# Text front end of a two-layer gated cross-attention kernel: mask plan first, queries for active tiles, key norms spread over later stages

## The chip, the core and the metric

The kernel runs on one core of one Trainium2 chip. The metric is the device time of one execution in microseconds (us). Three runs of the kernel before took 568.72, 568.03 and 567.38 us, median 568.03.

## What is computed

The activations `x` are 16 batches of 56 tokens of 128 numbers (896 tokens); the context `ctx` is 16 batches of 1500 keys of 128. Cut to what matters:

```
x = x + tanh(g_xattn[0]) * A0(layernorm(x), ctx, kv_mask, q_mask)
x = x + tanh(g_ffn[0])   * E0(layernorm(x))          # 16 experts, top 4, plus a shared one
x = x + tanh(g_xattn[1]) * A1(layernorm(x), ctx)     # slot attention, 3 iterations, GRU
x = x + tanh(g_ffn[1])   * E1(layernorm(x))          # 32 experts, top 2, capacity 68

A0:  q, k, v = x Wq, ctx Wk, ctx Wv                  # 16 heads of 64
     s = where(q_mask[i] & kv_mask[j], q k^T / 8, -max)
     out = softmax(s) v Wo + bout
A1:  keys are divided by rms(key) = sqrt(mean(key^2) + 1e-6)
```

Only a pair (query, key) that is set in both masks has a score of its own. The masks are the complements of random lengths, so few pairs are set. A query without any such key attends to all 1500 keys alike: its output is the mean of the keys through `Wv Wo`. So A0 needs three things of the context: the keys of the active blocks, the mean key of each batch, and (for A1 later) the sum of squares of every key.

## The kernel before

All of it is one program with one instruction stream for each engine, written out by hand, and semaphores between them. The order on an engine is the order of the code.

**Folding.** `Wq Wk^T` of each of the 16 heads is multiplied once (L1455, 32 matmuls of 64 rows, evicted by ACT in L785) into `G`, and `Wv Wo` into `MO`; `MS` is the sum of `MO` over the heads, a reduction on DVE (L1050). The weights arrive by four DMAs in `ld_attn`, and PE waits for all four.

**Layernorm.** `ln(k)` (L956 to L967 on DVE, L766 and L768 on ACT, L1429 to L1441 on PE) takes means by a matmul, subtracts, squares, takes variances by 14 one-column matmuls, a square root, a reciprocal, a diagonal matrix and a matmul that broadcasts it. The front end waits for all 28 constants that POOL writes (L594 to L632).

**Front end (L1443 to L1487 on PE).** After `ln(0)` and the folds, a loop over 16 steps `b` does two things at once. For head `b` it computes the queries of all 896 tokens (L1469, two halves of 448 columns, evicted by ACT, L791) into `tilesT`. For batch `b` the keys are loaded into one of four buffers `mctx` (L507, L532 to L536), POOL adds the 12 chunks of a row to six (L639) and to three (L642), PE sums them over the partitions (L1464), ACT squares all of them (L776, 1536 columns), and DVE reduces the squares (L996). The buffers, `msq` (two) and the semaphores `key_sq`, `key_ss`, `key_add`, `key_sum` tie these together.

**Plan.** Queries are cut in tiles of 8 tokens (7 tiles a batch), keys in 4 blocks of 375. A pair (tile of a batch, block) that has a set query and a set key is an *item*. DVE finds them between the key reductions: L1004 to L1015 (counts), L1018 to L1034 (lists), L1039 to L1041 (one-hot rows `hot_r`), and PE multiplies lists by one-hot rows at `b == 6` (L1484). The results (`item_bt`, `item_blk`, `item_dst`, the number of items and of tiles) are written at L1056 to L1063. The masks come by eight DMAs on SP's queue (L518, L519), behind seven loads of activations, weights and context.

**Items (L1510 to L1526 on PE).** A loop of two items a trip, two items ahead. For item `j` PE does: transpose of the probabilities of `j` (L1515), scores of `j+2` (L1498, and the mask by L1499), transpose of the result of `j-1` (L1504), and the product with the values of `j` (L1523). ACT: eviction of the transposed probabilities (L832), exponentials of `j+2` (L807, L808), eviction of a result (L815), and it also issues the DMA for the rows of item `j+1` (L820). DVE: `block_maximum(j+2)` (L1077, L1079, L1082, L1084), then `accumulate(j)` (L1088, L1091, L1093, L1097). POOL copies the 8 queries of 16 heads (L658) and makes the mask row (L659). SP loads the transposed keys (L544, L545). Loads have two buffers.

**Behind the items.** The output projection over the active tiles (L1541), `ln(1)`, the gate and 18 steps of layer 0's experts (L1561, L1570, L1595 on PE, L848 on ACT, L1178 and L1182 on DVE), the square root of all 192 columns of `sumsq` (L838) and its reciprocal (L1168), `ln(2)`, then layer 1. From `x_new` 2 on SP loads the keys of the first eight batches, transposed (L568) and plain (L572) in turn.

## Time and profile before

| quantity | us |
|---|---|
| three runs | 567.38, 568.03, 568.72 |
| the profiled execution | 568.96 |
| its span in the profile | 567.2 |
| PE busy in the span | 479.8 (85%) |
| DVE busy | 358.0 (63%) |
| ACT busy | 321.6 (57%) |
| POOL busy | 210.8 (37%) |

The profile is of one execution. A view of stretches gives each engine's busy time between two moments, with the granted clock of PE (1.00 is 2.4 GHz, half of that 1.2 GHz). A timeline lists instructions by start. A view of groups gives, for each line and engine, busy time, mean duration, and the idle time in front of it with what ended it. PEld is PE's loading of weights. A name ending in q is an engine's queue: what it issues or waits for.

### The profile page before, as it was taken

Reading aid. Unit: us, or ns where it says so; the run is one execution under the profiler, and the core shown is the slowest. Engines: PE = TensorE matmul, PEld = TensorE weight load, DVE = VectorE, ACT = ScalarE, POOL = GpSimd, SP = SyncE. Lnnn points to the kernel's source line nnn. Section 1 sums busy time; section 2 is a strip of 40 time slices with the busy share of each in tenths; the row PEclk is TensorE's granted clock in tenths of the full one; section 3 lists DMA queues with packets and bytes.
Section 4 is the critical chain, followed back from the end, with each engine's and each line's share of the span. In section 5 each row is a group of like instructions: output and inputs, shape, how many; then the busy total and the mean of one; then the engine's idle time right before and its main releaser. Section 6 shows DMA issues by size and latency. Waiting matters only on the chain.

```text
span 567.2 us, 17702 instructions
## 1 busy us (share of the span) xinstructions
PE 479.8 (85%) x6484; PEld 364.5 (64%) x6484; DVE 358.0 (63%) x1029; ACT 321.6 (57%) x959; POOL 210.8 (37%) x366
## 2 busy tenths in 40 slices
PE   4894988999796999879999998999998588489980
PEld 2531225566573454458999987899997458479980
DVE  0789964677627354458889888788888544023333
ACT  2564763555411122379999999899999240033330
POOL 8293862222420000034555445445544203602331
PEclk9996996999797799999999999999999988879996
DMA  8762643444149970600000498000000596120013
GB/s 333 251 222 97 209 165 101 136 138 141 48 160 418 356 93 1 259 40 2 4 3 17 185 365 319 4 4 3 0 0 3 200 426 283 50 78 21 26 31 106
DMA packets 30566, 75.17 MB, mean 133 GB/s; under 512 B 6669, under 2 KB 22078, under 8 KB 29486
## 3 DMA queue, kind: packets, MB, share of 16 engines
q1 hardware_dynamic: 26062, 62.47, 32.1%
q0 software_dynamic: 1424, 7.81, 3.7%
q10 hardware_dynamic: 3024, 4.13, 2.2%
q8 instruction: 38, 0.62, 0.5%
q14 instruction: 18, 0.15, 0.1%
HBM read 69.85 MB, written 4.54 MB: 131 GB/s over the span
## 4 chain that ended last, share of the span: by engine, by line
PE 39%; ACT 20%; DVE 18%; issue 8%; POOL 7%; DMA 5%; ACTq 1%; POOLq 1%; DVEq 0%; SPq 0%
ACT work L864 14%; PE ps L1561 5%; PE ps L1762 4%; PE ps L1469 4%; PE ps L1776 3%; PE ps L1595 3%; DVE ps L1200 2%; POOL xe_scratch L751 2%; PE ps L1423 2%; POOL rq L696 2%; PE ps L1616 2%; PE ps L1541 2%; DMA region<-in_ctx_blk 2%; PE ps L1644 2%; ACT work L881 2%
## 5 line engine op out<-in xcount | busy, mean ns | idle before, releaser
L864 ACT ACTIVATE work<-ps,nb,rkey 125x56 f32<-125x56 f32 x576 | 179.6, 514 | 4.6 <-DVE nb L1208 4.4
L1630 PEld LDWEIGHTS ps<-work,region 128*61 128x61 f32 (+1 forms) x2304 | 75.2, 136 | 8.2 <-issue 5.0
L1630 PE MATMUL ps<-work,region 128*61 128x56 f32 (+1 forms) x2304 | 76.3, 221 | 4.1 <-ACT work L864 3.7
L1644 PE MATMUL ps<-region,work 125*64 125x129 f32 x1152 | 73.5, 274 | 3.2 <-POOL work L715 1.9
L715 POOL TENSOR_TENSOR work<-work,rs 125x336 f32<-125x336 f32 x96 | 70.6, 756 | 3.8
L1644 PEld LDWEIGHTS ps<-region,work 125*64 125x64 f32 x1152 | 64.8, 136 | 4.6 <-POOL work L715 2.6
L1217 DVE TENSOR_REDUCE sm<-work 125x6 f32<-125x336 f32 x96 | 45.5, 492 | 17.5 <-ACT work L864 17.5
L1200 DVE TENSOR_REDUCE ps<-ps 125x6 f32<-125x336 f32 x96 | 44.4, 504 | 0.8 <-PE ps L1630 0.7
L1616 PE MATMUL ps<-GI,work 112*64 112x112 f32 (+3 forms) x288 | 34.7, 309 | 5.8 <-DVE work L1264 3.1
L708 POOL TENSOR_TENSOR rs<-rs,rkey 125x12 f32<-125x12 f32 x48 | 10.3, 215 | 75.7 <-DVE rs L1226 75.7
L1469 PE MATMUL ps<-xln,folded 128*128 128x448 f32 x64 | 29.9, 592 | 10.0 <-ACT region L791 10.0
L848 ACT ACTIVATE early_w<-ps 128x448 f32<-128x448 f32 (+1 forms) x18 | 9.8, 543 | 43.2 <-PE ps L1561 43.2
L757 POOL DMA_INDIRECT ys_scratch<-folded,yidx x17 | 16.3, 957 | 45.2 <-ACT folded L935 42.5
L776 ACT ACTIVATE region<-early_w 125x1536 f32<-125x1536 f32 x16 | 23.7, 1490 | 12.8 <-DVE sumsq L996 12.8
L639 POOL TENSOR_TENSOR region<-early_w 125x768 f32<-125x768 f32 x16 | 29.0, 1813 | 4.8 <-DMA early_w<-in_ctx 3.4
L996 DVE TENSOR_REDUCE sumsq<-region 125x12 f32<-125x1536 f32 (+1 forms) x16 | 27.7, 1746 | 3.3 <-ACT region L776 3.3
L1561 PE MATMUL ps<-xln,early_w 128*128 128x448 f32 x64 | 29.8, 595 | 0.0
L1469 PEld LDWEIGHTS ps<-xln,folded 128*128 128x128 f32 x64 | 11.3, 197 | 26.8 <-ACT region L791 19.3
L1178 DVE TENSOR_TENSOR early_w<-early_w,ps 128x448 f32<-128x448 f32 (+1 forms) x18 | 11.1, 619 | 23.5 <-ACT early_w L848 23.5
L807 ACT ACTIVATE early_w<-m_before,m_minus 128x1 f32 (+1 forms) x22 | 6.5, 295 | 31.8 <-DVE m_minus L1084 31.8
L1616 PEld LDWEIGHTS ps<-GI,work 128*64 128x64 f32 (+2 forms) x288 | 17.2, 134 | 11.4 <-issue 4.1
L642 POOL TENSOR_TENSOR work<-region 125x384 f32<-125x384 f32 x16 | 16.0, 999 | 20.2 <-PE ps L1464 19.1
(303 smaller groups left out, 999.2 us busy)
## 6 DMA issues: line engine op xcount, KB each, us to landing
region<-in_ctx_wide SPq DMA_DIRECT2D x16, 774.0 KB, 7.0
early_w<-in_ctx SPq DMA_DIRECT2D x16, 768.0 KB, 4.3
region<-in_w SPq DMA_DIRECT2D x6, 2048.0 KB, 19.8
region<-in_ctxT SPq DMA_DIRECT2D x16, 750.0 KB, 9.2
work<-in_ctxT_blk SPq DMA_DIRECT2D x22, 187.5 KB
early_w<-in_w POOLq DMA_DIRECT2D x1, 4096.0 KB, 12.4
region<-in_ctx_blk ACTq DMA_DIRECT2D x11, 192.0 KB, 2.8
early_w<-in_ctx_blk ACTq DMA_DIRECT2D x10, 192.0 KB, 2.5
```

The lines of the kernel that those rows point to most:

```text
L639: gp.tensor_tensor(padd6[:CP, :], mctx[k][:CP, 0:CC // 2 * 128], mctx[k][:CP, CC // 2 * 128:], ALU.add).then_inc(key_add, 1)
L715: gp.tensor_tensor(shares_of(p, a, h), shares_of(p, a, h), bcast(rs[:, a, c], S), ALU.mult).then_inc(a_att, 1)
L776: act.activation(msq[k % 2][:CP, :], mctx[k][:CP, :], ACT.Square).then_inc(key_sq, 1)
L864: i = act.activation(shares_of(p, a, h)[:, c, :], ps[:CP, 2 + 2 * h + a, c * S:(c + 1) * S], ACT.Exp, bias=nb[:, a, q:q + 1], scale=rkey[: ...
L996: v.tensor_reduce(sumsq[:, bass.ds(b, 1), :], msq[k][:CP, :].rearrange("p (a c d) -> p a c d", a=1, d=D), AX.X, ALU.add).then_inc(key_ss, 1)
L1200: v.tensor_reduce(ps[:CP, 2 + 2 * h + a, 400:400 + CH], ps[:CP, 2 + 2 * h + a, 0:CH * S].rearrange("p (c s) -> p c s", s=S), AX.X, ALU.max ...
L1217: v.tensor_reduce(sm[:, a, c], shares_of(p, a, h), AX.X, ALU.add).then_inc(a_sum, 1)
L1469: pe.matmul(ps[:, h, 0:HALF], G[:, b, :], xln[:, half(h)], start=True, stop=True).then_inc(qa_mm, 1)
L1561: mm = pe.matmul(ps[:p, 2 * (j % 2) + g, 0:HALF], w, xln[:, half(h)], start=True, stop=True)
L1616: mm = pe.matmul(out[r0:r1], w[:, r0:r1], x, start=start, stop=stop, **more)
L1630: mm = pe.matmul(ps[r0:r1, 2 + 2 * h + a, c * S:(c + 1) * S], keysT[:, s, c0 + r0:c0 + r1], qT[:, p, a * S:(a + 1) * S], start=True, stop= ...
L1644: mm = pe.matmul(ps[i * COL:(i + 1) * COL, bank, 0:KW], A[:CP, p % 2, i, h, c * S:c * S + COL], keys[:, 2 * p + i, h * CH + c, :], start=( ...
```

## The change

Constants: the loads of items get a ring of four buffers (`RING`), the first 16 items are written out (`FIRST`), and eight batches are `MEAN_ONLY` in the front end.

1. SP's queue starts with `xT`, the weights of the first fold, four batches, then the weights of the second fold. The eight mask loads are issued by ACT on its own queue. ACT runs a `Sqrt` on one column before its first wait for all constants.
2. PE's first means wait for one constant instead of 28. DVE makes the counts of the plan inside `ln(0)`, after the centring, and the one-hot rows before the last step of `ln(0)`; PE does folds and the rank matmuls in between. The lists follow `ln(0)`.
3. Queries are computed for one tile at a time, for the tiles that have items only (`head_queries(i, tile)`: 16 matmuls of 128 columns, four evictions of 512). The last tile is done always, the others in a loop over `tiles`.
4. POOL adds a batch once, to six chunks; the second addition is gone, and PE sums with two matmuls of 384 columns instead of one. Sums for batches 0 to 7 are in the front end, squares for none.
5. The second fold (`MO`) comes after the queries, straight before the items, and `MS` comes from eight matmuls instead of DVE's reduction.
6. Between items 0 to 15, batches 8 to 15 are worked on: at even `j` POOL's addition and ACT's squares, at odd `j` DVE's reduction of them and PE's sums. The two matmuls of `keep_d` and the scaling that follows are behind items 1 and 2. The reduction to `mean_rows` is behind the items. ACT issues no DMAs for items; SP does. The DMAs of `w13` and `w2p` are behind item 15 on POOL.
7. In the first 16 steps of layer 0's experts, ACT squares half a batch (768 columns) of the keys that layer 1 has loaded (`msq0`), and DVE reduces it one step later. The square root for these eight batches stands in front of `ln(2)` on ACT, the reciprocal inside `ln(2)` on DVE. SP loads all plain keys of the first eight batches before the transposed ones. POOL's `key_rms` is behind `x_new` 4.
8. Layer 1's late expert weights are waited for eight experts at a time instead of four.

```diff
@@ SP
+            for dst, name in ((wqT, "wqT"), (wkT, "wkT")):
+                sp.dma_start(dst, t[name]).then_inc(ld_attn[0], 16)
+            for k in range(KEY_BUFS):
+                load_batch(mctx[k], k, ld_mctx[k])
+            for dst, name in ((wvT, "wvT"), (wo, "wo")):
+                sp.dma_start(dst, t[name]).then_inc(ld_attn[1], 16)
...
+            for b in range(KEY_BUFS, MEAN_ONLY + 2):
+                load_later(b)
+            sp.wait_ge(items_ok, 2)
...
+            for j in range(FIRST):
+                if j == 2:
+                    sp.wait_ge(fold_mm, 9)
+                blk = block_of(j)
+                load_keysT(blk, j, j % RING)
+                load_rows(blk, j, j % RING)
+                if j in LOAD_AFTER:
+                    load_later(LOAD_AFTER[j])
...
@@ POOL
+            def key_adds(b):
+                k = b % KEY_BUFS
+                gp.wait_ge(ld_mctx[k], b // KEY_BUFS * 16 + 16)
+                gp.wait_ge(key_sum, b + 1)
+                gp.tensor_tensor(padd6[b % 2][:CP, :], mctx[k][:CP, 0:CC // 2 * 128], mctx[k][:CP, CC // 2 * 128:], ALU.add).then_inc(key_add, 1)
...
+            for j in range(FIRST):
+                item_queries(j + AHEAD, (j + AHEAD) % RING, (j + AHEAD) // RING * 32 + 32)
+                if j in SQUARES_AT:
+                    key_adds(SQUARES_AT[j])
...
@@ ACT
+            for r in range(TILES):
+                act.dma_start(km8[r * B:(r + 1) * B, 0:M], t["kv_mask"]).then_inc(ld_mask, 16)
...
+            act.activation(warm_up[:, :], eps_ln[:, :], ACT.Sqrt)
             act.wait_ge(const, CONSTS)
             ln(0)
...
+            def item(j, k):
+                act.wait_ge(pt_mm, j + 1)
+                act.wait_ge(o_mm, j + 4)
+                act.copy(PT[:KP].rearrange("p c r -> p (c r)"), ps[:KP, 2, 0:KC * 128]).then_inc(pt_ev, 1)
+                probabilities(j + AHEAD, k % 2)
+                keep_result(j)
...
+            for j in range(FIRST):
+                item(j, j % RING)
+                if j in SQUARES_AT:
+                    squares(SQUARES_AT[j])
...
+                if j < HALVES:
+                    act.wait_ge(ld_keys[j // 4], 32)
+                    act.wait_ge(key_ss, B - MEAN_ONLY + j + 1)
+                    act.activation(msq0[j % 2][:CP, :, :], keys[:, j // 2, half_batch(j), 0:D], ACT.Square).then_inc(key_sq, 1)
...
@@ DVE
+            ln(0, plan_counts, plan_places)
...
+            v.wait_ge(plan_list, 2)
...
+            v.sem_inc(items_ok, 1)
...
+            for j in range(FIRST):
+                block_maximum(j + AHEAD, j % 2)
+                if j in SUMS_AT:
+                    key_squares(SUMS_AT[j])
+                accumulate(j)
+                if j == 2:
+                    keep_scales()
...
@@ PE
+            ln(0, first_folds)
+            for q in range(2, 4):
+                fold(0, q)
+            pe.wait_ge(plan_rs, 1)
...
+            for b in range(2):
+                key_sums(b)
...
+                    for m in range(4):
+                        mm = pe.matmul(ps[:, q % 2, m * 128:(m + 1) * 128], G[:, 4 * q + m, :],
+                                       by_tile(xln[:, :])[:, tile, :, :], start=True, stop=True)
+                    mm.then_inc(qa_mm, 1)
...
+            pe.wait_ge(plan, PLAN_LISTS)
...
+            for b in range(2, 5):
+                key_sums(b)
+            head_queries(0, TILES - 1)
+            for b in range(5, 7):
+                key_sums(b)
             pe.wait_ge(items_ok, 1)
...
+            with pe.Fori(1, tiles) as i:
+                head_queries(i, bass.ds(pe.snap(TILES - 1 - i), 1))
+            key_sums(MEAN_ONLY - 1)
...
+            for pair in range(H // 2):
+                mm = pe.matmul(ps[:, ALL_BANK, 0:128], wvT[:, pair, :], wo[:, pair, :], start=(pair == 0), stop=(pair == H // 2 - 1))
+            mm.then_inc(fold_mm, 1)
+            for q in range(4):
+                fold(1, q)
+            pe.wait_ge(fold_ev, 9)
...
+            for j in range(FIRST):
+                item(j, j % RING, j // RING * 32, j // RING * 16)
+                if j in SUMS_AT:
+                    key_sums(SUMS_AT[j])
...
```

## Rows read from the trace of the kernel before

**Rows 1.** Stretches: from:to, length, then busy us of PE, PEld, DVE, ACT, POOL, granted clock.
```profile
50.00:83.90 33.90, 30.50 (x82) 10.54 (x83) 29.13 (x28) 24.47 (x33) 20.14 (x18) 0.94 0.55 183
...
83.90:147.20 63.30, 57.63 (x286) 36.45 (x286) 42.33 (x164) 31.44 (x102) 20.14 (x46) 0.92 0.46 131
```

**Rows 2.** Timeline of the front end (start us, duration us; in brackets idle before, releaser).
```profile
7.17 3.35 PE L1429 MATMUL ps<-xT,mean_w 128*128 128x448 f32 x4 [7.17 <-POOL before_b L632]
...
9.88 1.28 ACT L766 ACT_TABLE_LOAD   x1 [9.75 <-DVE ln_tiles L956]
...
11.80 3.15 PE L1434 MATMUL ps<-mean_w,ln_tiles 128*128 128x1 f32 x14 [1.28 <-ACT ln_tiles L766]
...
34.22 1.11 DVE L1018 TENSOR_SCALAR firstc<-prefix 112x4 f32<-112x4 f32 x1
...
46.48 0.21 DVE L1034 TENSOR_SCALAR lists_w<-btidx,lastc 112x1 bf16<-112x1 f32 x1
```

**Rows 3.** The key mask's loads on SP's queue: issue to landing, min/median/max.
```profile
DMA to landing us min/median/max: 7.2/8.1/9.0
```

**Rows 4.** Groups of the front end: busy us, mean ns | idle before, releaser.
```profile
L639 POOL TENSOR_TENSOR region<-early_w 125x768 f32<-125x768 f32 x16 | 29.0, 1813 | 4.8 <-DMA early_w<-in_ctx 3.4 <-POOL before_b L632 0.4
...
L996 DVE TENSOR_REDUCE sumsq<-region 125x12 f32<-125x1536 f32 (+1 forms) x16 | 27.7, 1746 | 3.3 <-ACT region L776 3.3
...
L776 ACT ACTIVATE region<-early_w 125x1536 f32<-125x1536 f32 x16 | 23.7, 1490 | 12.8 <-DVE sumsq L996 12.8
...
L1464 PE MATMUL ps<-work,early_w 125*16 125x384 f32 x32 | 13.1, 491 | 0.7 <-ACT folded L785 0.7
...
L1030 DVE CAST first_w<-firstc 112x128 bf16<-112x128 f32 x4 | 5.7, 1417 | 0.0
...
L1455 PE MATMUL ps<-region 64*128 64x128 f32 x64 | 5.3, 289 | 0.0
```

**Rows 5.** Timeline: first scores, first and last transposes of items, output projection.
```profile
83.91 0.87 PE L1498 MATMUL ps<-work 128*128 128x375 f32 x2 [2.21 <-POOL work L659]
...
87.35 1.00 PE L1515 MATMUL ps<-GI,work 128*125 128x128 f32 x3
...
144.10 0.49 PE L1515 MATMUL ps<-GI,work 128*125 128x128 f32 x3
...
152.27 9.46 PE L1541 MATMUL ps<-region,folded 128*128 x64
```

**Rows 6.** Timeline of items in their steady state, three engines.
```profile
124.86 0.29 ACT L807 ACTIVATE early_w<-m_before,m_minus 128x1 f32 x1 [0.96 <-DVE m_minus L1084]
...
125.70 0.27 ACT L815 COPY region<-ps 128x128 f32 x1
...
125.78 0.33 PE L1499 MATMUL ps<-work,ones_b 1*128 1x375 bf16 x1
...
126.16 0.48 ACT L832 COPY work<-ps 125x384 f32<-125x384 f32 x1 [0.18 <-issue]
...
126.29 0.23 DVE L1077 SCALAR_TENSOR_TENSOR m_before<-m_run,work 128x1 f32<-128x1 f32 x1 [0.48 <-PE ps L1499]
...
126.77 0.93 PE L1523 MATMUL ps<-region,work 125*128 125x128 f32 x6 [0.19 <-ACT work L832]
...
127.08 0.16 DVE L1082 TENSOR_TENSOR m_run<-m_block,m_before 128x1 f32<-128x1 f32 x1
...
127.53 0.49 PE L1515 MATMUL ps<-GI,work 128*125 128x128 f32 x3
...
127.56 0.29 ACT L807 ACTIVATE early_w<-m_before,m_minus 128x1 f32 x1 [0.92 <-DVE m_minus L1084]
...
128.59 0.33 PE L1499 MATMUL ps<-work,ones_b 1*128 1x375 bf16 x1
```

**Rows 7.** Timeline of layer 0's experts (a step of DVE) and of ACT in ln(2).
```profile
198.30 0.62 DVE L1178 TENSOR_TENSOR early_w<-early_w,ps 128x448 f32<-128x448 f32 x1 [1.17 <-ACT early_w L848]
...
232.34 1.26 ACT L766 ACTIVATE ln_tiles<-ln_tiles 128x448 f32<-128x448 f32 x2 [0.80 <-DVE ln_tiles L956]
```

More of the change, by code:

```diff
@@ L32 @@
 AHEAD = 2
+RING = 4
+FIRST = 16
+MEAN_ONLY = 8
+SQUARES_AT = {2 * k: MEAN_ONLY + k for k in range(B - MEAN_ONLY)}
+SUMS_AT = {2 * k + 1: MEAN_ONLY + k for k in range(B - MEAN_ONLY)}
+LOAD_AFTER = {0: 10, 1: 11, 5: 12, 7: 13, 9: 14, 11: 15}
+FOLD_BANK = ((4, 5, 6, 3), (4, 5, 6, 3))
+ALL_BANK = 0
+SUM_BANK = 7
+HALVES = 2 * MEAN_ONLY
 E0, F0, TOP0, ROUTE = 16, 64, 4, 2.5
@@ L283, in build_program @@
         ld_x = sem("ld_x")
-        ld_attn = sem("ld_attn")
+        ld_attn = [sem(f"ld_attn{f}") for f in range(2)]
         ld_small = sem("ld_small")
@@ L801, in _ @@
+            head_queries(0, TILES - 1)
+            act.wait_ge(items_ok, 1)
+            tiles = act.value_load(item_n[0:1, 1:2], min_val=2, max_val=TILES)
+            with act.Fori(1, tiles) as i:
+                head_queries(i, bass.ds(act.snap(TILES - 1 - i), 1))
+            act.wait_ge(fold_mm, 5)
+            act.copy(MS[:, :], ps[:, ALL_BANK, 0:128]).then_inc(fold_ev, 1)
+            for q in range(4):
+                fold(1, q)
             act.wait_ge(ld_small, 16 * SMALL)
@@ new lines, in plan_places @@
+            def plan_places():
+                v.wait_ge(plan_rs, 1)
+                step(v.tensor_reduce(bidx[:, :], bstep[:, :], AX.X, ALU.add))
+                step(v.scalar_tensor_tensor(btidx[:, :], bidx[:, :], -float(B), btidx[:, :], ALU.mult, ALU.add))
+                for b in range(KB):
+                    step(v.tensor_scalar(lists_w[:, b, 3:4], bidx[:, :], -1.0, float(TILES), ALU.mult, ALU.add), wait=False)
+                v.wait_ge(plan_rank, 2)
+                step(v.tensor_scalar(rank[:, :], prefix[:, :], ps[:BT, 2, 0:1], None, ALU.add))
+                for b in range(KB):
+                    v.tensor_scalar(hot_r[b][:BT, :], iota_r[:BT, :], rank[:, b:b + 1], active[:, b:b + 1],
+                                    ALU.is_equal, ALU.mult).then_inc(plan_hot, 1)
@@ L1437, in ln @@
                     keep_busy(2)
+                if meanwhile:
+                    meanwhile()
                 for h in range(2):
@@ L1487, in _, with lists @@
-            pe.wait_ge(items_ok, 1)
-            pe.wait_ge(plan_hot, KB + 1)
-            for h in range(2):
-                mm = pe.matmul(ps[:, 5 + h, 0:HALF], ones[:BT, :], keep_d[:BT, half(h)], start=True, stop=True)
-            mm.then_inc(keep_mm, 1)
+                        mm = pe.matmul(ps[:, q % 2, m * 128:(m + 1) * 128], G[:, 4 * q + m, :],
+                                       by_tile(xln[:, :])[:, tile, :, :], start=True, stop=True)
+                    mm.then_inc(qa_mm, 1)
+            def lists(parts):
+                for bank, col, items, left in parts:
+                    rows = 128 if bank == 6 else 1
+                    for blk in range(KB):
+                        mm = pe.matmul(ps[:rows, bank, col:col + items], left(blk), hot_r[blk][:BT, 0:items],
+                                       start=(blk == 0), stop=(blk == KB - 1))
+                mm.then_inc(plan_list, 1)
@@ L1525, in _ @@
-            last = pe.snap((n + 1) // 2 * 2)
+            for j in range(FIRST):
+                item(j, j % RING, j // RING * 32, j // RING * 16)
+                if j in SUMS_AT:
+                    key_sums(SUMS_AT[j])
+                if j == 1:
+                    pe.wait_ge(plan_hot, KB + 1)
+                    for h in range(2):
+                        mm = pe.matmul(ps[:, 5 + h, 0:HALF], ones[:BT, :], keep_d[:BT, half(h)], start=True, stop=True)
+                    mm.then_inc(keep_mm, 1)
@@ L1526, in _ @@
+            with pe.Fori(FIRST // RING, (n + RING - 1) // RING) as i:
+                for k in range(RING):
+                    item(pe.snap(i * RING + k), k, i * 32, i * 16)
+            last = pe.snap((n + RING - 1) // RING * RING)
             transpose_result(last)
```

464 lines of the change are left out of this document (218 added, 246 removed).

## The prediction

> **What bounds the kernel now.** I read the page first, then the stretches, then the timeline at the seams. Until 83.9 us the front end runs at the pace of PE and DVE together: between 50 and 83.9 PE is busy 30.5 of 33.9 us and DVE 29.1 [rows 1]. PE multiplies all 16 heads by all tokens, DVE reduces 16 batches of squares at 1.75 us [rows 4]. The first scores start at 83.91, the first transposes of an item at 87.35, those of the last (20th) at 144.10, the output projection at 152.27 [rows 5]. So 19 steps took 56.75, or 2.99 an item. PE is busy 57.6 of 63.3 us there [rows 1]; ACT, DVE and POOL have room. Behind 152.27 the change touches little. It therefore trades one stage for another: the front end loses 14 tiles' worth of queries for two and half of the norms' work, and the items receive that work in between. The question is what a pair of items then costs.
>
> **Front end.** I walk along the new order, in us from the start.
> - Means: PE need not wait, but DVE still waits for all constants, at 7.17 [rows 2]. Of ACT's two table loads the one of 1.28 in front of the squares goes [rows 2], since `Sqrt` is loaded early and squares run under it. Variances start at 8.5 instead of 11.80 and end at 11.7 (3.15, [rows 2]).
> - Counts: they need the masks. Eight issues on ACT end near 4. Behind SP's big loads the masks took 8.1 to land [rows 3]; the same would be 12.3 here, an immediate landing 6.5. I take 9.5, nearer the middle, because ACT's queue has nothing in front of them but the same DMA engines carry 2.2 MB. The counts take 4 to 6; 4.3 taken, to 13.8.
> - Reciprocal and diagonal 1.4, PE's broadcast 2.9 the four records took 3.35 in the cold start, like L1429 [rows 2], two folds at 0.66 (5.3 over 8, [rows 4]), rank: 20.0.
> - One-hot rows and the last multiplications of `ln(0)`: 3.3, to 23.3.
> - Lists: before, 34.22 to 46.69, 12.5 [rows 2]. Of this 5.7 are four copies of 128 columns at 1.42 each [rows 4], as long as the POOL additions beside them (1.8 and 1.0). After the change POOL starves there, since its third addition needs PE's sum and its fifth needs sums that stand behind the lists. Bounds 4 and 12.5; 5 taken, to 28.3. List matmuls 3.1, to 31.4.
> - Sums 2 to 4 with one addition of 1.8 between them. A sum is now two matmuls of 384 columns; one is two records and 0.82 (13.1 over 16, [rows 4]), 0.68 issued behind one another, so 1.35. Together 4.6, to 36.0.
> - Queries of a tile: 16 matmuls of 128 columns at 0.30 (9.46 for 32, [rows 5]), 4.7, and 1.5 more for the first tile since PE comes out of waits at half clock; sums 5 and 6 2.7; two register loads and a loop entry 2.2 (the idle in front of the first scores, [rows 5]); second tile 4.7; sum 7 1.35. To 53.2.
> - Eight matmuls for `MS` 2.4, four folds 2.6, last eviction 0.7: first scores at **59**, against 83.91. **-24.9.** Bounds: everything early 54, everything late 65.
>
> **A pair of items.** Even item `e`: squares on ACT, 1.49, and an addition on POOL, 1.81; odd item: a reduction on DVE, 1.75, and 1.35 of sums on PE [rows 4]. By sums alone PE would need 2 x 2.45 + 1.35 = 6.2, DVE 2 x 2.25 + 1.75 = 6.3. But the order of each queue closes a chain from the scores of `e` to those of `e+2`, read off [rows 6]:
> scores end to `block_maximum` 0.18 (126.11 to 126.29); maximum to exponentials 1.27 (to 127.56); exponentials to eviction of a result and its end 1.11 (124.86 to 125.97); **squares 1.45**; probabilities' eviction with its gap 0.58; to PE 0.13; values 0.76 (126.77 to 127.53); **sums 1.35**; transposes and scores 1.39 (127.53 to 128.92). Total 8.22 a pair. Without the two bold terms it is 5.4, which is below the measured 5.98. ACT's squares stand between the exponentials of `e` and the eviction that `e-1` waits for, and PE's sums between the values of `e-1` and the scores of `e+2`. Neither has cover. What waits behind: on ACT the eviction of `e-1`, on DVE `accumulate(e-1)` behind the reduction, on PE the transposed result behind `accumulate`.
>
> POOL's addition shares a port with DVE. In the front end each of the copies of L1030 lasted about as long as the POOL instruction beside it [rows 4]. The addition comes when the mask row is done, 1.0 after the scores; L1082 starts at that very moment (127.08, [rows 6]) and DVE was waiting first, so I let `block_maximum` through and the block of up to 1.8 fall on `accumulate`, which has room. The Trainium skill (GPSIMD Engine Reference, Specifications) says that GpSimd contends for SBUF with Vector instructions that have two SBUF inputs or run in a two-port mode. By that rule L1082, which has two, could as well be held, and this is one of the rivals below.
>
> I take 8.3 a pair. Eight pairs 66.4. The `keep` matmuls and their scaling, which stood in front of the items, add 3 (bounds 1 and 5). The last three steps run with four buffers and no wait for DMA: 2.65 each and a loop entry 1, 9. Sum 78.4 against 56.75: **+21.6**. Behind them the reduction of `mean_rows` comes late: **+0.6**.
>
> **Layer 0's experts.** ACT's half squares are 0.75 to 0.85 (half of 1.49), DVE's half reduction 0.9 (half of 1.75). DVE idles 1.17 in each step of 2.45 [rows 7], ACT more; so nothing, with 0.27 of cover left on DVE. If the cover is gone it costs up to 0.9 x 16. Squares ran behind `Silu` in `ln(2)` without a table load [rows 7], so none is added. The first steps wait for keys, which are now loaded first. `ln(2)` gets a square root ahead of its squares, but loses its table load behind them: 0 to +1. The reciprocal of half the columns leaves the way to the experts: -0.5 together.
>
> **Edits at nothing.** DMAs of items on SP: three issues of 0.35 in an item of over 2.6. `w13` and `w2p` later: some 40 us ahead of their use still. Late expert weights in eights: they start at the same moment and the eighth expert comes long after. Squares of half the batches moved behind: only what is said above.
>
> The masks' landing has a rule too. The Trainium skill (DMA: Bandwidth & Descriptors, Queues, rings and completion order) says that each DMA engine goes round-robin between the queue rows that have work, packet by packet. By it the masks would land near the lower bound and the first scores come 1 to 2 us earlier than in my sum.
>
> **Sum.** -24.9 + 21.6 + 0.6 - 0.5 = -3.2. The profiled execution took 568.96 for a span of 567.2 and lies 0.9 above the median of 568.03. So the changed kernel would be near 565 on either account; I set **564.5**, as item 0 now meets a PE at full clock (in the kernel before, the first transposes took 1.00 instead of 0.49 [rows 5, 6]).
>
> **Rivals.**
> 1. *The pairs overlap better.* If the chain is broken, for example as squares fit into waits, a pair costs 7.3 or down to the 6.3 of DVE's own work: 8 to 16 less, 548 to 556. For: neither engine is full. Against: the queues are in order. Chance 0.16.
> 2. *The front end comes early* (masks at once, lists without any block, warm clock): 54, so 559. Chance 0.10.
> 3. *Slower: the chain gets longer inside the pairs.* The place is PE and `block_maximum` between two scores. Either POOL's addition wins against L1082 (+1.6 a pair), or PE, which now waits for a quarter of the time, falls to its 1.2 GHz level, where the 3.5 of PE's share in the chain double. It did so after waits: the first transposes took twice their later time [rows 5, 6]. With 1.7 a pair the time is 578. It decides from 0.6 a pair on. Chance 0.20.
> 4. *The front end comes late*, at 64: masks with the full 8.1, lists at 9: 569.5. Chance 0.12.
> That the change doesn't do what it says (queries for two tiles): 20 items and two projections speak for it; the case is in 4.
> Forecast: 0.42, itself 559 to 569.
>
> **How the numbers follow.** Differences under 0.2%, 1.1 us, can't be told from none. Faster: 0.36 of the forecast, rivals 1 and 2, 0.62. Same: 0.06 of the forecast and 0.04 of rival 4, 0.10. Slower: 0.28. Both signs hold much, so the forecast's own range is 559 to 569; the range for 8 in 10 takes half of rival 1 and half of rival 3: 553 to 575.
>
> **What the changed profile would show.** First scores at 59 (54 to 65); the first to the seventeenth transposes 69 apart; between scores of even items 8.3, with ACT's square directly ahead of an eviction that PE waits for; last three items 2.65 apart; output projection near 149; experts still 2.45 a step. The forecast is wrong if pairs take under 7.5 or over 9, or if the first scores start outside 55 to 63.

## The result and the profile after

The changed kernel takes **563.18 us**, median of 6 runs (562.06 to 565.18), against 569.04 for the kernel before, run beside it on the same chip (6 runs, 567.38 to 569.85). The ratio is 0.9888, 95% interval 0.9868 to 0.9909: 1.1% faster, some 6 us. The profiled execution took 562.27 us for a span of 560.6. The prediction said 564.5, which is 3.5 below the 568.03 it started from; the measured gain is 5.9.

The page of the kernel after: its head and the busy shares.

```profile
span 560.6 us, 17255 instructions
PE 473.6 (84%) x6540; PEld 368.4 (66%) x6540; DVE 351.1 (63%) x1038; ACT 309.0 (55%) x945; POOL 195.2 (35%) x350
```

Its stretches (from:to, length, then busy us of PE, PEld, DVE, ACT and POOL, clock, share and rate of DMA), cut at the transposes of items 0, 16 and 19 and at the output projection: items 0 to 15 with their batches, the last three steps, what leads to the output projection.

```profile
61.75:127.06 65.31, 56.38 (x261) 31.93 (x261) 49.88 (x141) 34.57 (x91) 26.90 (x39) 0.95 0.49 149
127.06:140.60 13.54, 10.25 (x43) 6.55 (x43) 5.48 (x19) 3.57 (x11) 7.33 (x14) 0.75 0.47 158
140.60:147.50 6.90, 3.86 (x22) 2.69 (x21) 5.21 (x16) 3.70 (x11) 2.50 (x3) 0.94 0.00 1
```

The timeline at the seams (start, duration, engine and line, operands; in brackets idle before and who released it).

```profile
12.03 0.28 DVE L1056 CAST keepq<-qm 112x8 f32<-112x8 uint8 x1 [3.52 <-DMA qm<-in_q_mask]
...
22.63 3.27 DVE L1077 TENSOR_SCALAR early_w<-early_w,rank,active 112x448 bf16<-112x448 f32 x4
...
40.43 3.88 PE L1545 MATMUL ps<-xln,folded 128*128 128x128 f32 x32
...
58.49 0.90 PE L1588 MATMUL ps<-work 128*128 128x375 f32 x2 [0.69 <-ACT folded L823]
...
61.75 1.01 PE L1599 MATMUL ps<-GI,work 128*125 128x128 f32 x3 [1.02 <-ACT work L859]
...
127.06 0.59 PE L1599 MATMUL ps<-GI,work 128*125 128x128 f32 x3
130.23 1.62 PE L1588 MATMUL ps<-region,work 128*128 128x375 f32 x2 [2.58 <-POOL work L697]
...
140.60 0.49 PE L1599 MATMUL ps<-GI,work 128*125 128x128 f32 x3
...
147.51 10.24 PE L1638 MATMUL ps<-region,folded 128*128 x64
```

In the kernel before, the transposes of item 16 stand here:

```profile
135.93 0.49 PE L1515 MATMUL ps<-GI,work 128*125 128x128 f32 x3
```

Where the time goes, before against after, from these rows, [rows 5] and the same lines further down the two traces:

| event | before | after | difference | predicted |
|---|---|---|---|---|
| first scores | 83.91 | 58.49 | -25.4 | -24.9 |
| first transposes | 87.35 | 61.75 | -25.6 | |
| 17th transposes (item 16) | 135.93 | 127.06 | -8.9 | -4.1 |
| last transposes (20th) | 144.10 | 140.60 | -3.5 | -3.3 |
| output projection | 152.27 | 147.51 | -4.8 | -2.7 |
| means of `ln(1)` | 163.00 | 159.02 | -4.0 | |
| results of layer 0's experts in `xT` | 230.61 | 225.15 | -5.5 | -3.2 |
| means of `ln(3)` | 452.23 | 446.13 | -6.1 | |
| end | 567.2 | 560.6 | -6.6 | -3.2 |

So 25.6 us are gained ahead of the items and 22.1 of them given back between the items: 16.7 up to item 16 (65.31 for 48.58) and 5.4 in the last three steps (13.54 for 8.17). The chain of waits shows one pair of items in its steady state (start, duration, what):

```profile
89.51 0.28 PE ps L1589
...
89.81 0.22 DVE m_before L1119
90.03 0.47 DVE m_block L1121
...
90.97 0.28 ACT early_w L858
...
91.97 1.38 ACT region L828
93.36 0.38 ACT work L871
...
93.78 0.94 PE ps L1606 x6
94.71 1.39 PE ps L1518 x4
96.11 0.52 PE ps L1599 x3
96.63 0.63 PE ps L1588 x2
97.26 0.27 PE ps L1589
```

From 89.51 to 97.26 are 7.75 us. ACT's square (L828) stands between the exponentials and the eviction (L871) that PE's products (L1606) wait for, and PE's sums (L1518) stand before the next transposes. The products of odd items start at 86.03, 93.78, 101.53, 109.29, 117.04 and 124.80: the same 7.75 or 7.76 each time.

### The profile page after: what moved, and what is told of

The parts are those of the page before. It is cut to its first block, busy times and chain, and to the rows that moved or that the text cites. A ratio compares the mean times of both kernels' runs of the same rounds, so it can differ in the third digit from the quotient of the medians.

```text
span 560.6 us, 17255 instructions
## 1 busy us (share of the span) xinstructions
PE 473.6 (84%) x6540; PEld 368.4 (66%) x6540; DVE 351.1 (63%) x1038; ACT 309.0 (55%) x945; POOL 195.2 (35%) x350
## 4 chain that ended last, share of the span: by engine, by line
PE 40%; ACT 22%; DVE 19%; issue 7%; POOL 6%; DMA 3%; ACTq 1%; POOLq 0%; DVEq 0%; SPq 0%
ACT work L920 15%; PE ps L1658 5%; PE ps L1859 4%; PE ps L1873 3%; PE ps L1518 3%; PE ps L1692 3%; DVE ps L1262 2%; POOL xe_scratch L797 2%; PE ps L1484 2%; PE ps L1588 2%; PE ps L1638 2%; POOL rq L741 2%; PE ps L1606 2%; ACT region L828 2%; ACT work L937 2%
## 5 line engine op out<-in xcount | busy, mean ns | idle before, releaser
L1727 PEld LDWEIGHTS ps<-work,region 128*64 128x64 f32 (+1 forms) x2304 | 75.0, 137 | 7.7 <-issue 4.6
L1727 PE MATMUL ps<-work,region 128*64 128x56 f32 (+1 forms) x2304 | 76.0, 221 | 3.7 <-ACT work L920 3.7
L1119 DVE SCALAR_TENSOR_TENSOR m_before<-m_run,work 128x1 f32<-128x1 f32 x22 | 7.2, 326 | 34.8 <-PE ps L1589 34.8
L1658 PE MATMUL ps<-xln,early_w 128*128 128x448 f32 x64 | 27.5, 556 | 0.0
L858 ACT ACTIVATE early_w<-m_before,m_minus 128x1 f32<-128x1 f32 (+1 forms) x22 | 6.5, 297 | 31.4 <-DVE m_minus L1126 31.4
L681 POOL TENSOR_TENSOR region<-early_w 125x768 f32<-125x768 f32 x8 | 15.4, 1925 | 23.0 <-PE ps L1518 19.3
L696 POOL COPY work<-region 128x128 f32 x22 | 6.5, 295 | 47.1 <-DMA work<-in_kv_blk 19.0
L982 ACT COPY ln_tiles<-ps 128x512 f32<-128x512 f32 (+1 forms) x5 | 2.6, 522 | 36.3 <-PE ps L1838 36.3
L1658 PEld LDWEIGHTS ps<-xln,early_w 128*128 128x128 f32 x64 | 12.6, 198 | 12.5 <-issue 12.1
L1859 PE MATMUL ps<-ln_tiles,region 128*64 128x96 f32 x384 | 20.3, 248 | 0.0
## 6 DMA issues: line engine op xcount, KB each, us to landing
early_w<-in_w POOLq DMA_DIRECT2D x1, 4096.0 KB, 12.3
```

The costliest lines, as they stand in the source:

```text
L1658: mm = pe.matmul(ps[:p, 2 * (j % 2) + g, 0:HALF], w, xln[:, half(h)], start=True, stop=True)
L1727: mm = pe.matmul(ps[r0:r1, 2 + 2 * h + a, c * S:(c + 1) * S], keysT[:, s, c0 + r0:c0 + r1], qT[:, p, a * S:(a + 1) * S], start=True, stop= ...
L1859: mm = pe.matmul(ps[r0:r0 + COL, HIDDEN_BANK[e % DEEP], c * CAP:c * CAP + WIDE], weights(e)[:, c * 128 + r0:c * 128 + r0 + COL], xeT[:, e ...
```

## Experiments

My theory (A) is this chain. The rivals were that DVE's reduction sets the pair, that POOL's addition does by holding up DVE, or that PE's work alone does. Ratios are to the kernel before on the same chip, with 95% intervals; the changed kernel's is 0.9888 (0.9868 to 0.9909). The first four runs below were taken on one chip and the other eight on another, and a part that none of these edits touches differs: from the means of `ln(3)` to the end of the span took 115.0 us before and 114.5 in the changed kernel, 115.3 to 115.6 in the first four and 117.3 to 120.3 in the others. So times and spans are not compared across runs; I read the ratios, and the traces ahead of `ln(3)`.

**The square almost gone.**

```diff
-act.activation(msq[b % 2][:CP, :], mctx[b % KEY_BUFS][:CP, :], ACT.Square)
+w = CC * 128 if b < MEAN_ONLY + 2 else 8
+act.activation(msq[b % 2][:CP, 0:w], mctx[b % KEY_BUFS][:CP, 0:w], ACT.Square)
```

> Leaves out: ScalarE's squares between the items for batches 10 to 15 (8 columns instead of 1536; the first two stay whole, VectorE still reduces all 1536 columns, so the key norms of six batches are wrong). Theory A (the pair of items is a chain in which the square of 1.4 us stands ahead of the copy of the transposed P, and so ahead of the six product matmuls, which wait 1.0 to 1.2 us for it): the pair falls from 7.75 to about 6.5 us, six pairs, the kernel is 7 us faster (556). Theory B (VectorE's reduction of 1.74 us sets the pair, since it stands between the block maximum and the accumulation): the pair stays within 0.3 us of 7.75 and the time within 2 us. Theory C (the pair is simply the work of TensorE): no change.

Measured: 558.99, ratio 0.9815 (0.9773 to 0.9858), some 4 us below the changed kernel. From the products of item 3 to those of item 15 it takes 42.96 us (77.49 to 120.45) against 46.80 (78.00 to 124.80). The six pairs are 6.76, 6.67, 7.07, 8.86, 6.38 and 7.22. So the square is on the path, as A says. B (not within 0.3 of 7.75) is out as the whole cause, and so is PE's work alone, which is the same here. But the gain is 3.8 and not 7, and the pairs are uneven. The timeline of this kernel shows why, in the longest pair:

```profile
98.52 1.80 POOL L681 TENSOR_TENSOR work<-early_w 125x768 f32<-125x768 f32 x1
98.57 1.76 DVE L1125 TENSOR_TENSOR m_run<-m_block,m_before 128x1 f32<-128x1 f32 x1
```

A maximum of two single columns, 0.16 us otherwise, lasts as long as POOL's addition beside it, and the exponentials behind it come 1.6 us late. The pairs of 7.07 and 7.22 have such a hold too (1.19 and 1.33), the three of 6.4 to 6.8 have none.

**The reduction almost gone.**

```diff
-msq[b % 2][:CP, :].rearrange("p (a c d) -> p a c d", a=1, d=D)
+msq[b % 2][:CP, :].rearrange("p (a c d) -> p a c d", a=1, d=D)[:, :, :, 0:8]
```

> Leaves out: 15/16 of VectorE's reductions of the squares between the items (8 of 128 columns of each block are summed, batches 8 to 15). Theory A (the square on ScalarE holds the chain): pair stays at 7.75 us within 0.2, time within 1 us of the changed kernel. Theory B (VectorE's reduction holds it): pair 6.0 to 6.7 us, time 9 to 13 us lower.

Measured: 564.68, 0.9900 (0.9859 to 0.9940). The timeline, products of two odd items in a row:

```profile
86.51 0.94 PE L1606 MATMUL ps<-early_w,work 125*128 125x128 f32 x6 [1.20 <-ACT work L871]
94.27 0.94 PE L1606 MATMUL ps<-region,work 125*128 125x128 f32 x6 [1.20 <-ACT work L871]
```

7.76, and 7.75 to the next at 102.02. These two alone don't decide, since in each POOL's addition holds L1130 in the place of the reduction (1.84 us at 86.29, 1.63 at 94.08). But the pair from 111.56 to 119.30 has no hold over 0.6 us, DVE's 1.74 us are gone from it, and it takes 7.74. The reduction costs nothing where it stands; B is out. (The other two pairs, with slices at clock 0.79, are 9.54 and 9.39.)

**The additions almost gone.**

```diff
-gp.tensor_tensor(padd6[b % 2][:CP, :], mctx[k][:CP, 0:CC // 2 * 128], mctx[k][:CP, CC // 2 * 128:], ALU.add)
+w = CC // 2 * 128 if b < MEAN_ONLY else 16
+gp.tensor_tensor(padd6[b % 2][:CP, 0:w], mctx[k][:CP, 0:w], mctx[k][:CP, CC // 2 * 128:CC // 2 * 128 + w], ALU.add)
```

> Leaves out: GpSimd's additions of batches 8 to 15 between the items (16 of 768 columns). Theory A: GpSimd's additions cost the items nothing, since VectorE's maximum of two columns (the instruction that was held up to 1 us in the kernel before when an addition ran) shows a mean of 0.27 us here: pair 7.75, time within 1 us. Rival (the two engines hold each other, some 0.5 us a pair): 4 us lower.

Measured: 564.88, 0.9914 (0.9877 to 0.9951); pairs of 7.76 and 7.75 again (86.72, 94.48, 102.23, and 111.75 to 119.50); two with a drop of the clock are 9.52 and 9.39. So in the changed kernel the additions cost nothing. My reason for it in the expectation was wrong, though: they do hold DVE there (and what held L1082 in the kernel before, for 0.77 us at most, lay beside POOL's selections at 146.05, not beside an addition). In the changed kernel's timeline:

```profile
107.37 1.49 ACT L828 ACTIVATE region<-early_w 125x1536 f32<-125x1536 f32 x1
107.42 1.81 POOL L681 TENSOR_TENSOR region<-early_w 125x768 f32<-125x768 f32 x1
107.62 1.62 DVE L1119 SCALAR_TENSOR_TENSOR m_before<-m_run,work 128x1 f32<-128x1 f32 x1 [0.20 <-PE ps L1589]
108.76 0.48 ACT L871 COPY work<-ps 125x384 f32<-125x384 f32 x1
```

The held instruction ends at 109.24, while ACT was squaring until 108.8 and PE's products waited for ACT. Between 80 and 126 us the changed kernel has two DVE instructions held for over 0.9 us (1.62 and 1.33), this one none, and the period at full clock is the same. The square covers the hold; without the square (above) it shows.

**The sums almost gone.**

```diff
-for c in range(2): ... padd6[b % 2][:CP, c * CC // 4 * 128:(c + 1) * CC // 4 * 128]
+w = CC // 4 * 128 if b < MEAN_ONLY or b == B - 1 else 16
+for c in range(2): ... padd6[b % 2][:CP, c * CC // 4 * 128:c * CC // 4 * 128 + w]
```

> Leaves out: most of TensorE's row sums of batches 8 to 14 between the items (2 matmuls of 16 columns instead of 384; the last batch keeps its whole sums). Theory A (the sums stand between the products of one item and the transposes of the next, which wait for nothing else): the pair falls by most of 1.46 us, to 6.4 to 6.8, the time by 6.5 to 9 us. Rival (the next transposes or products wait anyway for ScalarE or VectorE, so that the sums fill an idle stretch): less than 3 us.

Measured: 561.73, 0.9860 (0.9806 to 0.9913): not clear of the changed kernel, where 6.5 to 9 us were expected. Pairs where the clock is full: 6.70 (104.14 to 110.84), 7.56 and 7.30. The first is what A gives; in the other two L1124 is held by the addition again (1.33 and 1.30 us), and with the sums gone the transposed result waits 1.19 and 0.93 us for DVE, whose reduction had been running beside the sums. PE, less busy, also worked at half clock for part of the items (0.57 in the slice 93 to 101; the three earlier pairs took 8.4 to 9.5). So by these three pairs the sums are on the path, at 0.2 to 1.0 us a pair rather than 1.4; the waits say that DVE's reduction is right behind them.

**The square one wait earlier.** Nothing left out.

```diff
 def item(j, k):
     ...
     act.copy(PT[:KP].rearrange("p c r -> p (c r)"), ps[:KP, 2, 0:KC * 128]).then_inc(pt_ev, 1)
+    if isinstance(j, int) and j in SQUARES_AT:
+        squares(SQUARES_AT[j])
     probabilities(j + AHEAD, k % 2)
     keep_result(j)
 ...
     item(j, j % RING)
-    if j in SQUARES_AT:
-        squares(SQUARES_AT[j])
```

> Nothing is left out: the square of a batch stands behind the copy of the transposed P and ahead of the exponentials of the item two ahead, in the 1.6 us in which ScalarE waits for VectorE's maximum, instead of behind the item. Theory A (the pair is a chain through the square and the copy behind it): the pair falls from 7.75 to 6.4 to 7.2 us, the kernel by 4 to 10 us against the changed one. What may hold it above 6.4: VectorE's maximum meets GpSimd's addition, as in the run with the short squares (1.76 us instead of 0.16). Rival (the square only moves the wait to the exponentials): pair within 0.3 of 7.75, time within 2 us.

Measured: 560.36, 0.9823 (0.9766 to 0.9879). In its trace:

```profile
95.64 0.48 ACT L871 COPY work<-ps 125x384 f32<-125x384 f32 x1 [0.84 <-PE ps L1599]
96.02 1.49 ACT L828 ACTIVATE region<-early_w 125x1536 f32<-125x1536 f32 x1
97.83 0.29 ACT L858 ACTIVATE early_w<-m_before,m_minus 128x1 f32<-128x1 f32 x1 [0.32 <-DVE m_minus L1126]
...
105.22 1.80 POOL L681 TENSOR_TENSOR region<-early_w 125x768 f32<-125x768 f32 x1
105.71 1.32 DVE L1119 SCALAR_TENSOR_TENSOR m_before<-m_run,work 128x1 f32<-128x1 f32 x1 [0.49 <-PE ps L1589]
```

The square now ends before the exponentials could start (0.32 us of idling left where the changed kernel idles 1.6). Pairs: 8.16, 7.56, 6.59, 6.48, 7.26, 7.28. In the first, PE waits 1.79 us for DVE behind the scaling of `keep`, and nothing is gained (8.03 in the changed kernel). The next three long ones each begin with a hold of 1.3 to 1.5 us, as in the last two rows; the two without one are 6.5. From first scores to output projection: 83.0 us against 89.0. By the trace 6.0 us are gained in that stretch, and they are still there at `ln(3)` (440.12 for 446.13); by the ratios it is 3.7, and the two intervals overlap a little. The gain between the items is shown, its size in the total less surely.

**Additions beside the reduction.** On top of the last edit.

```diff
-if j in SQUARES_AT:
-    key_adds(SQUARES_AT[j])
+if j - 1 in SUMS_AT:
+    gp.wait_ge(m_neg, j + 2)
+    key_adds(SUMS_AT[j - 1])
 ...
-if j in SUMS_AT:
-    key_sums(SUMS_AT[j])
+if j - 1 in SUMS_AT:
+    key_sums(SUMS_AT[j - 1])
+if j == FIRST - 1:
+    key_sums(B - 1)
```

> Nothing is left out. As the run with the square behind the copy of P, and GpSimd starts a batch's addition when VectorE has taken the maximum ahead of its reduction, so that the addition lies beside the reduction (one SBUF input) and no longer beside VectorE's small instructions with two SBUF inputs; TensorE's sums come one item later. Theory (what held the pair at 6.5 to 7.6 in that run is the addition, which holds such an instruction of 0.16 us for up to 1.8): pair 6.1 to 6.5 us in every pair, no such instruction above 0.6 us between the items, 3 to 6 us below that run. Rival (the sums and the two items alone make 7 us): the same pair as there, time within 1 us, or higher if the later queries hold TensorE.

Measured: 574.75, 1.0022 (0.9998 to 1.0045): as slow as the kernel before, where 3 to 6 us below the last run were expected. While an addition lies beside a reduction no DVE instruction is held for over 0.6 us; the one hold left (1.14 us at 128.74) is beside the last addition, which has no reduction beside it. So the holds do come from the addition, and still the version is worse. Two rows say why:

```profile
83.04 0.49 PE L1596 MATMUL ps<-GI,work 128*128 128x128 f32 x2 [1.78 <-DVE work L1141]
84.13 2.60 PE L1520 MATMUL ps<-work,early_w 125*16 125x384 f32 x4
```

Reduction and sums used to run beside each other behind an odd item. Moved to the even one, the sums (1.46) cover nothing, and the reduction leaves PE 1.78 us idle. A pair without a clock drop is 7.99 (88.90 to 96.89); behind such a wait the sums can run at half clock (2.60), and the four pairs from 9.62 to 9.85 all have such a drop. In their old place the sums covered the reduction; I had not seen that.

**Masks ahead of the batches.**

```diff
+sp.wait_ge(ld_mask, 16 * (TILES + 1))
 for k in range(KEY_BUFS):
     load_batch(mctx[k], k, ld_mctx[k])
```

> Nothing is left out: SyncE issues the first four batches and the weights behind them only when the masks have landed. Theory (the masks, issued by ScalarE by 4.4 us, land at 12.0 because the batches' 3 MB are ahead of them or beside them): they land at 7 to 9, the counts start behind the centring at 8.6 to 9.5, and first scores come 2.5 to 3.4 us earlier (55 to 56), the batches' additions later at no cost. Rival (the masks are slow by themselves, 1500 bytes a row and eight DMAs in a row): landing stays near 12, no gain, first scores as before or later. The time follows: 2 to 4 us lower, or 0 to 2 higher.

Measured: 565.49, 0.9889 (0.9844 to 0.9934): no gain in the total. The trace of it:

```profile
8.22 2.02 SPq L525 DMA_DIRECT2D early_w<-in_ctx  x4
...
8.67 0.17 DVE L1057 CAST keepq<-qm 112x8 f32<-112x8 uint8 x1
...
56.02 0.90 PE L1589 MATMUL ps<-work 128*128 128x375 f32 x2 [0.69 <-ACT folded L824]
...
73.55 1.82 POOL L682 TENSOR_TENSOR region<-early_w 125x768 f32<-125x768 f32 x1
73.59 1.79 DVE L1155 TENSOR_TENSOR gate_bout<-bout,gates 128x1 f32<-128x1 f32 x1
```

The masks are there by 8.22 instead of 12.0, and the counts start 3.4 us earlier: it was the traffic of the batches and of the weights behind them that made them late. First scores come 2.5 us earlier. Then 3.5 us are lost in the items: the addition now meets the first instruction of the scaling of `keep` (1.79 us, 0.14 in the changed kernel), TensorE waits 1.97 us for DVE at 81.24 (0.46 in the changed kernel) and works at half clock behind it. That this collision took all of the gain in every run I can't show from one profile.

**Weights of the experts behind the loop.**

```diff
-gp.wait_ge(key_sq, B - MEAN_ONLY)
-gp.wait_ge(key_sum, B + 2)
-gp.dma_start(w13, t["w13"]).then_inc(ld_ffn0, 16)
-gp.dma_start(w2p, t["w2p"]).then_inc(ld_ffn0, 16)
 with gp.Fori(FIRST // RING, (n + RING - 1) // RING) as i:
     ...
+(the four lines here)
```

> Nothing is left out: GpSimd issues the load of layer 0's expert weights behind the loop of the items instead of ahead of it. Theory (the first item in the loop waits 2.6 us for GpSimd, whose two DMA issues of 0.78 and 0.56 us stand ahead of the queries of item 18 and themselves wait for the last sums; and the idle TensorE drops to 1.2 GHz for the first item behind it): the wait falls below 1 us, the slow matmuls (1.62, 1.49) go back to 0.80 and 0.83, last products 3 to 5 us earlier, time 3 to 5 us lower; the weights still land 30 us ahead of their use. Rival (the entry of the loop costs this much on any engine): within 1 us.

Measured: 561.42, 0.9825 (0.9749 to 0.9900). The two issues in the changed kernel, ahead of the queries of item 18:

```profile
127.80 0.78 POOL L707 DMA_DIRECT2D early_w<-in_w  x1 [7.38 <-PE ps L1518]
128.59 0.56 POOL L708 DMA_DIRECT2D early_w<-in_w2p  x1
```

The seam of items 15 and 16 with the issues behind the loop:

```profile
126.88 0.94 PE L1606 MATMUL ps<-region,work 125*128 125x128 f32 x6 [1.18 <-ACT work L871]
...
130.88 0.83 PE L1606 MATMUL ps<-region,work 125*128 125x128 f32 x6
```

From products to products it takes 4.00 us, 7.99 in the changed kernel (124.80 to 132.79); to the last products 11.96 against 18.89. The wait for POOL is gone and so is the half clock. Of the 6.9 us 1.6 are used up by a drop of the clock between items 9 and 10 (5.64 from products to products, 4.00 otherwise), and 2.1 go back at once, since POOL's selections for the router (3.60 us in one row) then lie on the last accumulation: the last products are 5.9 us ahead of the output projection, not 3.8. From first scores to output projection 3.1 us remain, by the ratios 3.6, with intervals that overlap.

**TensorE kept busy ahead of the items.**

```diff
+def fill(n):
+    for _ in range(n):
+        pe.matmul(ps[:, 2, 0:256], mean_w[:, :], xT[:, 0:256], start=True, stop=True)
+pe.wait_ge(fold_ev, 7)
+fill(2)
 pe.wait_ge(fold_ev, 9)
 for k in range(AHEAD):
     item_scores(k, k, 32)
+fill(2)
```

> Nothing is left out; added are two matmuls of 256 columns on TensorE between the last two fold evictions and two more behind the first two scores, both where it waits for ScalarE and VectorE. Theory (the first items run at 1.2 GHz, 61.8 to 68, because TensorE idles 0.7, 1.0 and 1.3 us ahead of them): the granted clock stays at full from 53 to 70, the first transposes take 0.6 instead of 1.0 and products 0.83 instead of 1.49, 1.5 to 3 us lower. Rival (the clock falls for another reason, such as the half-empty matmuls of the folds or chance): no change of the durations, time within 1 us or 0.5 higher for the fillers.

Measured: 568.45, 0.9939 (0.9904 to 0.9974): no gain, and by the ratios 3 us slower than the changed kernel, at the edge of the intervals. The fillers do what they should:

```profile
62.00:70.00 8.00, 6.55 (x33) 4.22 (x34) 6.16 (x18) 5.71 (x17) 5.60 (x8) 1.00 0.54 148
64.75 0.90 PE L1612 MATMUL ps<-region,work 125*128 125x128 f32 x6
69.02 0.94 PE L1612 MATMUL ps<-early_w,work 125*128 125x128 f32 x6 [1.20 <-ACT work L871]
```

The clock stays full (0.61 between 62 and 70 in the changed kernel) and the first products take 0.90, not 1.49. But those of item 1 start at 69.02, at 68.83 in the changed kernel. From first scores to there it takes 9.22 us, 10.34 in the changed kernel, so a warm PE wins 1.1 us there, and no more, since it then waits 1.20 for ACT's square. But first scores start 1.3 us later, since fillers stand ahead of them. Behind that, the addition meets the scaling of `keep` as with the masks ahead (L1154 held for 1.79 at 76.34), and the pair from 78.28 takes 9.52 for 8.03. The trace is 1.5 us late at the output projection (149.01) and 0.3 at `ln(3)`; the rest of the 3 us it doesn't show.

**Queries for all seven tiles.**

```diff
-with pe.Fori(1, tiles) as i:
+with pe.Fori(1, TILES) as i:
 (the same in ScalarE's program, and in the two waits for qa_ev)
```

> Undoes one part: the queries are computed for all seven tiles instead of the two that are active; masks, plan and items stay as in the changed kernel, and the output projection stays at two tiles. Theory (the front end ends when the last tile's queries are out of PSUM, 4.68 us a tile): first scores 5 x 4.68 = 23.4 us later, near 82, time 584 to 588, slower than the kernel before by 3 %. Rival (the queries hide behind the loads and additions of the batches, as they did in part before): less than 15 us later.

Measured: 591.34, 1.0300 (1.0227 to 1.0373): the 3% that was expected. First scores at 81.18, 22.7 us later than at 58.49, the five tiles at 4.5 each. So with all tiles the new front end is only 2.7 us shorter than the old, the norms moved away included; 22.7 of the 25.4 us hang on the tiles that are left out.

**The norms beside layer 0's experts.** Squares and reductions of 8 of 128 columns.

> Leaves out: 15/16 of the squares and reductions of the first eight batches beside layer 0's experts (8 of 128 columns, so these norms are wrong). Theory (a step of the experts is 2.45 us of TensorE; VectorE, with 0.94 us more in each, keeps 0.3 us idle): step 2.45 with and without, time within 1 us. Rival (the work costs what the step has grown to): 16 x 0.2 to 0.5, so 3 to 8 us lower.

Measured: 566.91, 0.9920 (0.9887 to 0.9953), not below the changed kernel. A step in this kernel:

```profile
186.43 0.92 PE L1692 MATMUL ps<-early_w 128*128 128x448 f32 x2
187.02 0.62 DVE L1232 TENSOR_TENSOR early_w<-early_w,ps 128x448 f32<-128x448 f32 x1 [1.06 <-ACT early_w L898]
...
188.88 0.92 PE L1692 MATMUL ps<-early_w 128*128 128x448 f32 x2
```

and the same in the changed kernel:

```profile
187.41 0.92 PE L1692 MATMUL ps<-early_w 128*128 128x448 f32 x2
188.00 0.62 DVE L1232 TENSOR_TENSOR early_w<-early_w,ps 128x448 f32<-128x448 f32 x1 [0.31 <-ACT early_w L898]
189.19 0.94 DVE L1239 TENSOR_REDUCE sumsq<-early_w 125x6 f32<-125x768 f32 x1
189.86 0.92 PE L1692 MATMUL ps<-early_w 128*128 128x448 f32 x2
```

2.45 us both times. The work fits into DVE's idle time, of which 0.31 us a step is left. It is free, as forecast.

**All together**, with the aligned additions: square earlier, masks ahead, weights behind the loop.

> Nothing is left out. The square behind the copy of P, the aligned additions, the masks ahead of the batches, the experts' weights behind the loop, together. If the gains add: front 3 us, pairs 8 x 1.4 = 11 us, loop entry 4 us, so 545 to 549 against 563 for the changed kernel. If one eats another (the front's 3 us were lost again in the items of the run with the masks ahead): 551 to 555.

Measured: 567.25, 0.9884 (0.9819 to 0.9949): the same as the changed kernel, and neither of the times that were expected (545 to 549, 551 to 555). Against the run with the aligned additions beside it (1.0022) this is 1.4% less, some 8 us for the masks and the weights' load, more than the two had brought singly (0 and 3.6). But it includes the alignment, which cost 2.0% on top of the earlier square (1.0022 for 0.9823), some 11 us. The same without the alignment was not run; what it would take stays open. Of the kernels that leave nothing out, the earlier square and the later load of the weights have the lowest ratios, 0.6 to 0.7% below the changed kernel, and both intervals still overlap its own.

## Why the prediction was right, step by step

The time (564.5 against 563.18) and the balance up to the last transposes (-3.3 against -3.5) are right, and so are the two mechanisms that carry it: the front end shrinks with the tiles, and a pair grows by the square and the sums. The terms beneath them are not all as good. That the balance at the last transposes comes out so near is luck, since two errors of 4 us cancel (at item 16 it was -8.9 for -4.1). Behind it 3.2 us more were gained than forecast: 1.9 up to the output projection and 1.0 in layer 0's experts, both below, and 1.1 behind the experts, less 0.8 in the projection itself (10.24 for 9.46), of which no run says more.

- **Front end, -24.9 against -25.4.** The queries went from seven tiles to two ("14 tiles' worth" in the prediction is a slip; its sum has two tiles). Variances at 8.50 as forecast. The masks came at 12.0, at my late bound (12.3) and not at the 9.5 I took. The Trainium skill (DMA: Bandwidth & Descriptors, Queues, rings and completion order) says the engines serve the queue rows that have work in turn, from which I inferred that a separate queue could bring them early; this trace does not bear the inference out, with 7.6 us from issue to landing. With the batches held back, they were there within 4.1. The 2.5 us lost there, 0.9 in the one-hot rows and the end of `ln(0)` (4.2 for 3.3; L1077 alone 3.27 with two additions beside it) and 1.8 in the lists' matmuls (4.9 for 3.1, the clock at 0.66) came back in other terms: counts 3.9 instead of 4.3, lists 3.8 instead of 5 (the copies of L1088 take 0.22, not 1.42, with POOL idle, as argued), the first tile 3.9 instead of 6.2, and no cost of the loop entry, where I had 2.2: PE was busy right up to it.
- **The pair, 8.3 against 7.75.** The chain is the one that was written down, link by link: scores to maximum 0.04 (0.18 forecast), maximum to exponentials 1.16 (1.27), to the square 0.90 (1.11), square 1.38 (1.45), eviction and gaps 0.53 (0.71), products 0.86 (0.76), sums 1.40 (1.35), transposes and scores 1.49 (1.39). The runs with a short square and with short sums show both bold terms on the path (6.4 to 6.8 without the square, 6.70 in the one pair without sums that no hold delays); the reduction and the addition cost nothing, as forecast. The mechanism was right, the links around the new work were 0.5 us too long.
- **Items 0 to 15: 65.3 from transposes to transposes, 69.4 forecast.** Eight pairs of 7.75 make 62.0 for 66.4, and 3.3 are left for the `keep` matmuls and the cold start, where I had 3.
- **Last three steps, 9 forecast, 13.5 measured.** This term failed. I put the loads of `w13` and `w2p` among the edits at nothing, by asking whether they come in time for their use, and did not ask what is queued behind them on POOL: the queries of item 18, for which PE waited 2.58 us and then ran at half clock (1.62 for 0.80). In the run with the loads behind the loop the same three steps take 7.7 us (129.14 to 136.85).
- **Item 0 at full clock**, as I argued for the last 0.8 us of the forecast: false. The transposes took 1.01, like [rows 5], and the clock was 0.61 from 62 to 70. By the run with the fillers this is worth some 1.1 us, so the step from 565 to 564.5 had no ground.
- **`mean_rows`, +0.6 forecast; the stretch behind the last transposes lost 1.3 instead** (8.17 to 6.91). By the traces its wait is POOL's selections, 3.60 us in both kernels: they started at 146.05 before, behind the last transposes at 144.10, and at 139.62 now, ahead of them. In the run with the loads behind the loop they again start behind them (138.40 and 136.85), and the stretch takes 7.90. I read no row of that stretch.
- **Layer 0's experts, -0.5 forecast, about -1.5 measured** between `ln(1)` and `x_new`. Steps 2.45, as forecast. The steps until full pace took 7.86 us before (184.96 to 192.82, clock 0.63) and 6.76 now (180.65 to 187.41, clock 0.73); the reciprocal ahead of them 1.35 and 0.75. Why the clock recovers earlier here was not tested.
- **Rival 3** did not happen, though half of its mechanism did: POOL's addition does win against small DVE instructions with two SBUF inputs, the counterpart of L1082 among them (L1124, 1.33 us at 116.20), but the period stays 7.75 through both holds. Its other half, half clock inside the pairs, stayed away: the clock is 1.00 from 80 to 126. The Trainium skill (GPSIMD Engine Reference, Specifications) names just this contention; the trace agrees (1.62 for 0.22, 1.33 for 0.16 us), and DVE's reduction, with one SBUF input, takes its 1.74 beside an addition as without. **Rival 1** would have needed the queues to be broken, which the change does not do and the earlier square does. **Rivals 2 and 4**, the front end at 54 or 64, did not come: 58.49.

## What to carry to other kernels

Work put between the steps of a pipeline costs what it adds to the chain that closes there, not its busy time: of four new pieces the reduction and the addition were free where they stood, and the square and the sums lengthened every pair. Place each in a wait that its engine has anyway, and keep pieces beside each other that cover one another; when one is moved away from a cover (here the sums from the reduction, to keep the addition off DVE's small instructions), the other becomes the wait. And a DMA issue is an instruction in a queue: ask what stands behind it on its engine, not only when its data are needed. When an edit shifts the phase of two engines, look again for collisions: two runs here gave gains back to one that was not there before.

## What the runs showed of the hardware

A DVE instruction of 0.14 to 0.26 us on one column, with two inputs in SBUF, was held for up to 1.84 us (the run with the short reduction) while POOL added 768 columns (1.80 to 1.82); which instruction it hit differed between kernels that differ there only in phase, and where DVE was the late one it cost most of the hold, as in the run with the masks ahead (6.03 us from the products of item 3 to those of item 4, 4.53 in the changed kernel). Small loads on a queue of their own took 7.6 us beside 3 MB of batches and the weights behind them on another queue, and at most 4.1 with these held back. And TensorE's granted clock fell to half inside the items in some kernels and not in others, behind waits of 1.7 to 2.6 us for instance, but not behind each (1.79 us at 82.66 in the run with the earlier square, full clock after it), and also where PE had waited only 1.20 us (the sums of 2.47 us at 103.10 in the run with short additions); the cause of a single drop stays open. A drop was worth 1.6 to 1.8 us (a pair of 9.39 or 9.54 in place of 7.75), as much as most edits tried here.
